# Joined changes in the first layer's loop of a two-layer cross-attention kernel, and its first weights rounded within the last product evictions

## The reference

```
# layer 0 (16 heads of 16)
q = LN1(x) @ Wq;  k, v = split(LN2(ctx) @ Wkv)
x = x + softmax(q k^T * 0.25) v @ Wproj + bproj
x = x + gelu(LN3(x) @ W1 + b1) @ W2 + b2          # hidden 1024
# layer 1 (16 heads of 64)
x = x + attention(LN(x), LN(x)) @ Wo1 + bo1        # self-attention, 512 tokens
x = x + attention(LN(x), ctx) @ Wo2 + bo2
a, g = split(LN(x) @ Wp + bp);  x = x + (a * gelu(g)) @ Wf + bf
```

## Time and profile before

| | us |
|---|---|
| median of 3 runs | 2342.82 (2341.16 to 2347.05) |
| the profiled execution | 2332.97 |
| its span | 2331.20 |
| TensorE busy | 2135.2 (92%) |
| VectorE busy | 1627.0 (70%) |
| ScalarE busy | 1449.5 (62%) |
| GpSimd busy | 1104.8 (47%) |

### The profile page before, as it was taken

One profiled execution on the slowest core, in us unless ns is written; L12 is line 12 of the kernel. 1 busy time (PEld: TensorE's weight loads), 2 busy tenths in 40 slices (PEclk: granted clock), 3 DMA queues, 4 the chain that ended last, 5 costly groups with the idle time before them and its releaser, 6 DMA issues. The chain is left out here.

```text
span 2331.2 us, 31301 instructions
## 1 busy us (share of the span) xinstructions
PE 2135.2 (92%) x11628; PEld 1780.3 (76%) x11628; DVE 1627.0 (70%) x2353; ACT 1449.5 (62%) x2098; POOL 1104.8 (47%) x867
## 2 busy tenths in 40 slices
PE   6867999997799999999999999999998799999998
PEld 4655778786577787777777777777876689889987
DVE  6566667664578777787777878778776866666553
ACT  5444666654477777777777777777775354545431
POOL 2145455543145444454454544545444675566432
PEclk8968999999999999999999999999999999999999
DMA  7710000011000000100001000010013411111000
GB/s 237 264 41 5 21 21 21 10 48 46 28 24 15 24 24 15 37 15 24 24 14 33 18 23 26 15 33 15 17 37 130 162 46 55 55 55 46 10 10 19
DMA packets 84280, 102.67 MB, mean 44 GB/s; under 512 B 29664, under 2 KB 61152, under 8 KB 83616
## 3 DMA queue, kind: packets, MB, share of 16 engines
q1 hardware_dynamic: 84128, 100.66, 12.9%
HBM read 65.50 MB, written 33.82 MB: 43 GB/s over the span
## 5 line engine op out<-in xcount | busy, mean ns | idle before, releaser
L146 PE MATMUL PS<-R 128*128 128x512 f32 (+1 forms) x2944 | 1028.6, 349 | 98.9 <-DVE R L162 55.9
L147 PE MATMUL PS<-R 128*128 128x512 f32 (+1 forms) x2944 | 999.2, 339 | 0.0
L148 PE MATMUL PS<-R 128*128 128x512 f32 (+1 forms) x2944 | 998.9, 339 | 0.0
L146 PEld LDWEIGHTS PS<-R 128*128 128x128 f32 x2944 | 567.4, 193 | 213.3 <-DVE R L162 70.2
L156 ACT ACTIVATE R<-PS 64x512 fp32r<-64x512 f32 (+4 forms) x860 | 460.3, 548 | 275.6 <-PE PS L1768 129.4
L148 PEld LDWEIGHTS PS<-R 128*128 128x128 f32 x2944 | 567.0, 193 | 61.1
L147 PEld LDWEIGHTS PS<-R 128*128 128x128 f32 x2944 | 568.3, 193 | 54.9
L162 DVE TENSOR_TENSOR R<-F,R 128x1024 fp32r<-128x1024 f32 (+2 forms) x416 | 478.6, 1156 | 44.1 <-ACT R L156 22.3
L159 POOL TENSOR_SCALAR R<-F 128x512 fp32r<-128x512 f32 (+1 forms) x343 | 294.8, 862 | 347.2 <-DVE F L1921 147.0
L1463 ACT ACTIVATE F<-PS 128x1024 f32<-128x1024 f32 x256 | 262.9, 1027 | 177.5 <-DVE R L162 122.3
L159 POOL TENSOR_SCALAR R<-R 64x512 fp32r<-64x512 f32 x128 | 143.0, 1131 | 391.4 <-ACT R L156 391.4
(11 more groups left out here) (90 smaller groups left out, 1983.5 us busy)
## 6 DMA issues: line engine op xcount, KB each, us to landing
F<-sd SPq DMA_DIRECT2D x128, 128.0 KB, 2.8
xs<-F SPq DMA_DIRECT2D x16, 512.0 KB, 2.6
F<-xs SPq DMA_DIRECT2D x16, 512.0 KB, 3.6
gd<-F SPq DMA_DIRECT2D x8, 768.0 KB, 3.5
vd<-F SPq DMA_DIRECT2D x8, 768.0 KB, 5.7
R<-gd SPq DMA_DIRECT2D x6, 1024.0 KB, 5.6
R<-vd SPq DMA_DIRECT2D x6, 1024.0 KB, 5.6
F<-in_x SPq DMA_DIRECT2D x8, 512.0 KB, 4.9
```

The costliest lines, as they stand in the source:

```text
L146: nc.tensor.matmul(o, L[0], Rr[0], start=start, stop=False, skip_group_check=share)
L147: nc.tensor.matmul(o, L[0], Rr[1], start=False, stop=False, skip_group_check=share)
L148: return nc.tensor.matmul(o, L[1], Rr[0], start=False, stop=stop, skip_group_check=share)
```

## The change

At p = 7 ScalarE rounds `g1[0:2]` behind the first `vs5` eviction and `g1[2:4]` behind the second; VectorE takes its remainders of them ahead of that of `vr5`, and those of jobs 4 and 5 behind the keys' (ScalarE rounds 4 and 5 ahead of the keys' copies). In iterations 0 to 9 the odd chunks' scores go to banks 6 and 7, and the norm transposes too; the scores then wait for the differences two chunks back, the query for those of the last even chunk, the transposes for those of i - 1. ScalarE makes all 64 roundings of the hidden layer, right behind the gelu of each, and GpSimd none.

```diff
@@ -593,6 +593,9 @@
                     for i in (0, 2):
                         act.wait_ge(vw5_mm, 4 * p + i)
                         act_copy(vs5[p % 2][:, 2 * i:2 * i + 2, :], vw5_bank(i)).then_inc(vw5_act.sem, 1)
+                        if p == 7:
+                            for job in g1[i:i + 2]:
+                                act_weight(job)
                     act.wait_ge(vw5_mm, 4 * p + 3)
                     act_copy(vr5[p % 2][:, :, 0, :], vw5_bank(3)).then_inc(vw5_hi.sem, 1)
 
@@ -638,6 +641,9 @@
                             nc.vector.tensor_copy(g5_view(gs5[p % 2], 1), g5_bank(1)).then_inc(g5_dve.sem, 1)
                         hi, lo = [g5_view(gr5[p % 2][:, :, h, :], k) for h in range(2)]
                         dve_rest(lo, g5_bank(k, 0, 2), hi).then_inc(g5_lo.sem, 1)
+                    if p == 7:
+                        for job in g1[:4]:
+                            dve_weight_rest(job)
                     dve.wait_ge(vw5_hi, p)
                     dve_rest(vr5[p % 2][:, :, 1, :], vw5_bank(3), vr5[p % 2][:, :, 0, :]).then_inc(vw5_dve.sem, 1)
 
@@ -679,9 +685,7 @@
         av0_mm, o0_hi, o0_lo = event("d_mm", 2 * NB), event("o_hi", 2 * NB), event("o_lo", 2 * NB)
         o0_mm, o0_add = event("o_mm", 2 * NB), event("x_add", 2 * NB)
         up_mm, gelu, h_lo, down_mm = [event(n, NM) for n in ("up_mm", "gelu", "h_lo", "down_mm")]
-
-        NPOOL = 2 * (N0 + 2 - LAG0)
-        h_hi, h_act = event("h_hi", NPOOL), event("h_act", NM - NPOOL)
+        h_hi = event("h_hi", NM)
         res = event("res", 2 * NB)
 
 
@@ -696,6 +700,14 @@
         norm0_at = {"x": (0, P_LN1W, P_LN1B), "g": (0, P_LN3W, P_LN3B), "s": (2, P_G1, P_B1)}
 
         turn_bank = (2, 5)
+
+        def score_bank(c):
+
+            return 6 if c < LAG0 and c % 2 == 1 else 0
+
+        def norm0_bank(i):
+            return 6 if i < LAG0 else 0
+
         first1 = (N0 + 7, N0 + 8, N0 + 9, N0 + 11)
 
         def norm0_to(kind, b):
@@ -755,7 +767,7 @@
             def query(b):
                 pe.wait_ge(ln_nl, number0["x", b])
                 wait_weights(pe, "q")
-                pe.wait_ge(sc0_sub, 4 * b - 1)
+                pe.wait_ge(sc0_sub, 4 * b - 2 if 4 * b - 1 < LAG0 else 4 * b - 1)
                 for g in range(2):
                     for k in range(2):
                         m = mm3(bank(g), [v[:, k, 128 * g:128 * g + 128] for v in W0q], [v[:, k, :] for v in ns[b % 2]],
@@ -782,11 +794,11 @@
                 b, q = divmod(c, 4)
                 pe.wait_ge(q0_lo, 2 * b + 1)
                 pe.wait_ge(k0_in[b % 2], b // 2)
-                pe.wait_ge(sc0_sub, c - 1)
+                pe.wait_ge(sc0_sub, c - 2 if c <= LAG0 else c - 1)
                 if c - 1 in norm0:
                     pe.wait_ge(ln_aff, 2 * norm0[c - 1][2] + 1)
                 for g in range(2):
-                    m = mm3(bank(g), [v[:, g, 128 * q:128 * q + 128] for v in Q1], [kd_b[b % 2][:, hl, g, :] for hl in range(2)],
+                    m = mm3(bank(score_bank(c) + g), [v[:, g, 128 * q:128 * q + 128] for v in Q1], [kd_b[b % 2][:, hl, g, :] for hl in range(2)],
                             True, True)
                 m.then_inc(sc0_mm.sem, 1)
 
@@ -863,8 +875,8 @@
                 if i % 2 == 0 and ok((i - 4) // 2, 2 * NB):
                     project((i - 4) // 2)
                 if i in norm0:
-                    pe.wait_ge(sc0_sub, min(i, N0 - 1))
-                    ln_transpose(norm0[i][2], 0)
+                    pe.wait_ge(sc0_sub, i - 1 if i < LAG0 else min(i, N0 - 1))
+                    ln_transpose(norm0[i][2], norm0_bank(i))
                 if ok(n + 1, NM):
                     up(n + 1)
                 if i % 4 == 2 and ok((i - 2) // 4, NB) and i > 2:
@@ -919,10 +931,10 @@
             def rounds(n):
                 act.wait_ge(gelu, n)
                 act.wait_ge(down_mm, n - 3)
-                act_copy(h1[n % 3][0], hf1[n % 3]).then_inc(h_act.sem, 1)
+                act_copy(h1[n % 3][0], hf1[n % 3]).then_inc(h_hi.sem, 1)
 
             act.wait_ge(g5_mm, 15)
-            for job in g1:
+            for job in g1[4:]:
                 act_weight(job)
             for g in range(2):
                 act.wait_ge(kt_mm, g)
@@ -940,7 +952,7 @@
                     act_weight(job)
                 if ok(n, NM):
                     gelus(n)
-                if NPOOL <= n < NM:
+                if ok(n, NM):
                     rounds(n)
                 if ok(i, N0):
                     act.wait_ge(sc0_sub, i)
@@ -949,13 +961,13 @@
                     query(i // 4 + 1)
                 if i in norm0:
                     kind, b, k = norm0[i]
-                    ln_affine(k, norm0_at[kind][1], norm0_at[kind][2], 0)
+                    ln_affine(k, norm0_at[kind][1], norm0_at[kind][2], norm0_bank(i))
                 if i + 1 in norm0:
                     kind, b, k = norm0[i + 1]
                     ln_scale_act(k, xbuf(norm0_at[kind][0], b))
                 if ok(n + 1, NM):
                     gelus(n + 1)
-                if NPOOL <= n < NM:
+                if ok(n + 1, NM):
                     rounds(n + 1)
                 if i % 2 == 1 and ok((i - 3) // 2, 2 * NB):
                     m_ = (i - 3) // 2
@@ -1005,27 +1017,24 @@
 
             def largest(c):
                 dve.wait_ge(sc0_mm, c)
-                nc.vector.tensor_reduce(mx4, heads(bank(0, 2)), AX.X, ALU.max).then_inc(sc0_max.sem, 1)
+                nc.vector.tensor_reduce(mx4, heads(bank(score_bank(c), 2)), AX.X, ALU.max).then_inc(sc0_max.sem, 1)
 
             def differences(c):
                 dve.wait_ge(sc0_max, c)
                 dve.wait_ge(w_lo_pool, [j.rest for j in g1 if j.by_pool][-1])
                 dve.wait_ge(t0_mm, 2 * (c - 3) + 1)
-                nc.vector.tensor_tensor(heads(E1[c % 3]), heads(bank(0, 2)), mx4.unsqueeze(2).to_broadcast([128, 16, 64]),
+                nc.vector.tensor_tensor(heads(E1[c % 3]), heads(bank(score_bank(c), 2)), mx4.unsqueeze(2).to_broadcast([128, 16, 64]),
                                         ALU.subtract).then_inc(sc0_sub.sem, 1)
 
             def rests(n):
-                if n < NPOOL:
-                    dve.wait_ge(h_hi, n)
-                else:
-                    dve.wait_ge(h_act, n - NPOOL)
+                dve.wait_ge(h_hi, n)
                 dve_rest(h1[n % 3][1], hf1[n % 3], h1[n % 3][0]).then_inc(h_lo.sem, 1)
 
-            for job in g1:
-                dve_weight_rest(job)
             for g in range(2):
                 dve.wait_ge(kt_hi, g)
                 dve_rest(KT[:, 1, g, :], bank(4 + g), KT[:, 0, g, :]).then_inc(kt_lo.sem, 1)
+            for job in g1[4:]:
+                dve_weight_rest(job)
             query(0)
             value(0)
             for i in loop0:
@@ -1087,11 +1096,6 @@
                     next(ahead)
 
         def pool_attention0(ahead):
-            def rounds(n):
-                pool.wait_ge(gelu, n)
-                pool.wait_ge(down_mm, n - 3)
-                pool_copy(h1[n % 3][0], hf1[n % 3]).then_inc(h_hi.sem, 1)
-
             def divided(c):
                 pool.wait_ge(rec0, c)
                 ev = E1[c % 3].rearrange("p (h s) -> p h s", h=16)
@@ -1116,12 +1120,8 @@
                     divided(i - 1)
                 for job in weights0_at(i):
                     pool_weight(job)
-                if ok(n, NPOOL):
-                    rounds(n)
                 if LAG0 <= i - 1 < N0:
                     divided(i - 1)
-                if ok(n + 1, NPOOL):
-                    rounds(n + 1)
                 if i in norm0:
                     kind, b, k = norm0[i]
                     if kind == "g":
```

## The result

The changed kernel takes 2313.57 us (median of 4 runs, 2311.70 to 2314.34), the kernel before beside it 2341.99 (4 runs). The ratio is 0.9876, interval 0.9856 to 0.9896: 28.4 us less by the medians (29.0 by the ratio), where 22.1 were forecast. The profiled executions differ by 21.3 (2311.70 against 2332.97). The last product matmul ends at 93.58 us of the trace before and at 99.30 of the one after. The same stage ends between 93.5 and 94.5 or between 98.8 and 99.9 in all fourteen traces of this study, with the old border of the stages and with the new.

A forecast was written before the change was run, and what follows sets the result against it. TensorE was taken to bound the loop, and the order of work the stretch ahead of it. The parts 5.0 + 8.2 + 7.4 + 1.5 = 22.1 us, off the median 2342.82, gave 2320.7, range 2308 to 2334.

The forecast's parts named there:

- case of 16 to 28 us: The whole kernel: the forecast itself, 16 to 28 us faster, chance 0.57.
- the period gains more: Layer 0's loop: rival, fewer waits keep the clock up in the middle periods; over 28 us, about 2311; chance 0.08.
- A: Border before the loop: first weights rounded within evictions, key product 2.2 us earlier; gain 5.0, ends 2.0 and 5.3.
- B: Iterations 0 to 9: second score and norm banks, gains 3.5 (iterations 2 to 4) and 4.7 (6 to 8); 8.2.
- C: Steady loop: hidden rounding on ScalarE ends waits behind GpSimd's roundings; 1.85 us in each of four periods, 7.4.
- D: Loop's end: GpSimd's split or add leaves two VectorE remainders, 1.1 each; second rounding costs 0.65 once; gain 1.5.
- the first scores near 106: Border: sign that first scores start near 106 us instead of 111.11, 6.6 behind the key copies' issues; wrong after 109.
- The other wait of the period: Before the value and norm statistics: ScalarE 0.65 us later, VectorE no longer held back 0.8; gain nil.
- the clock falls no more in the middle periods: Middle periods, before at 0.93 and 2 us longer: rival's claim that fewer waits keep the clock up; chance 0.08.
- The lock: Steady loop: GpSimd's moved norm remainder holds back VectorE's next remainder through shared SBUF ports by about 0.4; sum 1.6 less.
- ScalarE becomes the bound: Loop: rival, both roundings of an iteration fall on the turned copies' path; 18 us slower, about 2361; chance 0.05.
- Clock and locks take a part: Border, query stretches, loop: rival, half clock stays and GpSimd's moved work holds VectorE; gain 7 to 16, chance 0.22.

The follow-up runs named there:

- e6: Kernel before, with only the odd chunks' scores of iterations 0 to 9 in second banks, norm transposes in the old ones; 2330.11 us, ratio 0.9959.
- e2: Kernel before, with only the second banks for scores and norm transposes in iterations 0 to 9; 2326.34 us, ratio 0.9948.
- e3: Kernel before, with only the hidden layer's rounding moved, all on ScalarE; 2326.15 us, ratio 0.9951.
- e11: The changed kernel once more, unaltered, timed beside the kernel before; 2315.84 us, ratio 0.9886.
- e5: Kernel before, GpSimd keeping its 48 hidden roundings but behind the division, norm's split and bias add of the iteration; 2328.77 us, ratio 0.9956.
- e4: The changed kernel with each hidden rounding done twice on ScalarE, the second waiting for the first; 2335.77 us, ratio 0.9984.
- e7: The changed kernel with four of sequence 0's first eight key copies issued from ScalarE's queue; 2312.12 us, ratio 0.9879.
- e1: Kernel before, with only the first weights rounded within the evictions; 2333.43 us, ratio 0.9988.

## Why the prediction was right, and where its sizes were off

The direction was right and the time lies in the range of 2308 to 2334. The size lies at the upper end of the forecast's own case of 16 to 28 us: 28.4 by the medians is just over it, 27.0 by the marks just under it, and the measurement can't tell it from the case "the period gains more". The sizes of the parts erred both ways: to the loop's end the pair of traces gives A 3.1, B 11.9, C 13.9 and D 0.8, 29.6 against 22.1, and 4.7 of C is clock, which the sum did not count. The three parts alone give 2.8, 12.2 and 11.5, in sum 26.5 against 29.0 together by the same measure, each known to 3 or 4 us. By the marks they add more closely: chunk 0 gains 3.2 with A alone and 3.1 with all, chunks 0 to 9 gain 11.6 and 11.9, a period 2.3 in both. No sign of overlap shows.

**A: 5.0 forecast, 3.1 in the pair of traces.** The step to the key product was right: 0.90 us after the products, at 2.4 GHz, and the issues 5.0 earlier (5.3 worked out). The failed step is "the first scores near 106" from a fixed 6.6 behind the issues. Issue to scores took 7.24 instead of 6.61: sixteen issues now take 10.98 instead of 10.33. They begin 1.4 us after the last stores were issued (105.20 against 102.32 + 1.49), before it was 6.4. The forecast had 0.3 for that. The DMA lines above show the stores moving at 396 GB/s while the first four copies are issued, with 2.8 us to their landing instead of 1.9; no run takes the stores away, so the cause is likely but not shown. The other 1.3 is the clock, and there the trace I read was the exception, not the new kernel. Against the four later traces of the old border A gives 4.1 to 4.3, which with the 0.6 is close to the forecast.

**B: 8.2 forecast, 11.9 in the pair, 11.6 alone.** The place and cause were right: both gains fall at the query products. Iterations 6 to 8 gave 5.3 (4.7 forecast), iterations 2 to 4 gave 6.3 (3.5). The mis-sized term is the second. I credited it with the earlier start alone, 3.5; the query product came 3.9 earlier beyond A and also ran at 2.4 GHz, and with it the output and the next scores. Of the two reasons I gave for the start, the query's own wait for the differences carries nearly all: e6 keeps the norm's old banks, with ScalarE's wait of 0.97 still there, and gains 4.9 from chunk 3 to 4. The norm's banks, which I named first, give 1.1 at chunk 3 (0.97 worked out), and from chunk 2 to 4 e2 gains only 0.5 more than e6.

**C: 7.4 forecast.** The waits of 0.64 and 1.07 went, with VectorE's 1.54, and are worth 1.6 a period against 1.85 forecast. The other wait of the period, which I put at nil, gives 0.2. The term that the sum lacks is the remainder beside GpSimd's other bias add, 0.5: in all 2.3 a period and 9.2 in four. What is left of the 11.7 (e3), 11.5 (e11) or 13.9 (full, chunks 11 to 27) comes nearly all in steps of 1.9 to 2.2, and these are clock. Such steps stand in A alone, which touches nothing there, at the same chunks: 2.1 at 16 and 2.1 at 20. B alone has none, e6 has both (2.2 and 1.7), e11 one. So the rival "the clock falls no more in the middle periods" describes what the full kernel's trace shows (0.93 to 1.00), but the cause it names, fewer waits, is not it: A alone keeps 19.9 us of TensorE's waits for remainders (207 to 489 us of its trace) and still gets both steps. Before, the granted clock is 0.50 from 281 to 287 and 0.52 from 335 to 342; in A alone it is 0.51 from 281 to 284 only, and 1.00 from 336 to 343. The two traces of the changed kernel differ in the same way: chunks 19 to 23 take 50.3 in the first and 52.5 in e11, with 0.50 from 316 to 322. What decides it remains open. So 4.7 us of the pair's gain was luck of the traces as far as these runs show.

The idle of VectorE before its shift went as worked out, and e5 confirms the mechanism. The lock: the norm remainder that the prediction meant now stands as follows, timeline after.

```profile
390.89 2.40 POOL L165 TENSOR_TENSOR R<-F,R 128x1024 fp32r<-128x1024 f32 x1
...
392.78 0.69 DVE L162 TENSOR_TENSOR R<-PS,R 128x512 fp32r<-128x512 f32 x1 [1.95 <-ACT R L156]
...
393.39 0.68 DVE L162 TENSOR_TENSOR R<-F,R 128x512 fp32r<-128x512 f32 x1
```

The remainder of VectorE that starts beside it reads PSUM and takes 0.69; the one with both inputs in SBUF starts 0.10 after its end and takes 0.68. The other norm's is alike (413.05, with VectorE's 0.71 from PSUM at 414.18). The 0.4 a period that I put on it did not appear. At the loop's end the pair still shows, timeline after:

```profile
510.71 2.39 POOL L1136 TENSOR_TENSOR F<-F 128x1024 f32<-128x1024 f32 x1
510.76 2.35 DVE L276 SCALAR_TENSOR_TENSOR F<-F 128x4 f32<-128x4 f32 x1 [0.91 <-POOL F L256]
```

A shift that takes 0.15 elsewhere ends with GpSimd's add. The Trainium skill, SBUF — State Buffer (Who interferes with whom), has the shared ports as an exclusive lock, and the trace agrees in this place (2.35 us), as it does in the 1.19 beside the bias add of before; my estimate from it failed since I did not look at which operation would stand beside the moved one.

**D: 1.5 forecast, 0.8 in the pair, 1.9 to 2.0 in e3 and e11** (chunk 27 to the loop's end). The two waits shrank by 1.1 each, as worked out (1.80 to 0.70, 1.55 to 0.43). The pair loses 1.7 from chunk 27 to 28, where the new kernel's granted clock is 0.51 from 420 to 427 us; e3 and e11 lose nothing there. The loop as a whole ended 29.6 earlier, where under 15 would have refuted the forecast, and a period takes 50.3 (chunks 19 to 23), under the 51 to 52 foretold; without a slow spell it took 52.7 before (chunks 11 to 15).

**What the rivals were worth.** "ScalarE becomes the bound" did not come; ScalarE has no cover for one more rounding of each block (e4). "Clock and locks take a part" happened at the first scores (1.3) and was outweighed by clock gained at both queries.

## What to carry to other kernels

Where an engine works in order, look first at what stands behind its longest wait: letting GpSimd round last was worth as much in the steady loop as taking 48 roundings from it. Before crediting a change with an earlier start, see which of the waiting instruction's inputs is freed, and price the matmuls behind the start at the clock they will then run at. Compare traces from a mark that both share, and take more than one trace of the kernel before: here the reference trace was 1.0 to 1.2 us ahead at chunk 0 of four variants with the same border, and the last product matmul ended 5.7 us apart in the two traces.

## What the runs showed of the hardware

- TensorE's slow spells in a steady loop come and go with no change to the kernel (full and e11). A spell of 6 to 7 us at 1.2 GHz costs a period of four chunks some 2.2 us (52.5 against 50.3), one of 3 us 0.2 (50.5 against 50.3). Of two long ones, one was cut to 3 us and one was gone when only the border of the stages had changed and the loop ran 4.7 us earlier (e1).
- The length of the idle alone did not set the level of the next matmul: 0.47 after 3.45 us of idle (e7), 0.77 after 2.06 to 2.27 (the old border in e2, e3, e5 and e6). In e7 the matmuls then slowed at 112.00, 1.5 us into the scores.
- Sixteen small key copies take 10.3 to 11.0 us to issue from one queue, about 0.67 each; taking four of them to a second queue ended the issue of the first eight 2.3 us sooner and brought the first scores forward by 1.4, with stores still moving.
- ScalarE's change of table costs its load and nothing beside it. Timeline of e4, where no wait follows:

```profile
416.15 1.30 ACT L156 ACTIVATE R<-F 128x512 fp32r<-128x512 f32 x2
...
417.46 1.28 ACT L962 ACT_TABLE_LOAD   x1
418.76 1.06 ACT L962 ACTIVATE F<-F 128x1024 f32<-128x1024 f32 x1
```

The load stands right behind the rounding and the exponential 1.30 after its start. The Trainium skill, ScalarE: Activation LUTs (What ACT_TABLE_LOAD costs), has the same 1283 ns and a drain of some 1380 ns more; the second doesn't show here.
